# One more product by C on GpSimd, one more product by B per group of states on ScalarE

## What is computed

```python
def _selective_scan(u, delta, A, Bm, Cm, Dp):
    def step(h, inp):
        u_t, d_t, b_t, c_t = inp
        dA = jnp.exp(d_t[:, :, None] * A)
        h = dA * h + (d_t * u_t)[:, :, None] * b_t[:, None, :]
        y = jnp.einsum('bdn,bn->bd', h, c_t)
        return (h, y)
    ...
def _mamba_block(x, p):          # 4 layers; 256 inner channels, 16 states
    xn = _rmsnorm(x, p['norm_w'])
    xp, z = jnp.split(xn @ p['Win'], 2, axis=-1)
    xc = jax.nn.silu(_causal_depthwise_conv(xp, p['conv_w'], p['conv_b']))
    dt, Bm, Cm = jnp.split(xc @ p['Wx'], [DT_RANK, DT_RANK + D_STATE], axis=-1)
    delta = jax.nn.softplus(dt @ p['Wdt'] + p['bdt'])
    y = _selective_scan(xc, delta, -jnp.exp(p['A_log']), Bm, Cm, p['Dp'])
    return x + (y * jax.nn.silu(z)) @ p['Wblk']
```

## Time and profile before

| | |
|---|---|
| median of 3 runs | 2149.23 us (2148.23 to 2153.09) |
| the profiled execution's own time | 2150.92 us |
| its span in the trace | 2149.1 us |
| VectorE busy | 1940.8 us, 90% |
| GpSimd busy | 1457.5 us, 68% |
| ScalarE busy | 1683.6 us, 78% |
| TensorE busy | 1868.8 us, 87% |

### The profile page before, as it was taken

One profiled execution on the slowest core, in us unless ns is written; L12 is line 12 of the kernel. 1 busy time (PEld: TensorE's weight loads), 2 busy tenths in 40 slices (PEclk: granted clock), 3 DMA queues, 4 the chain that ended last, 5 costly groups with the idle time before them and its releaser, 6 DMA issues.

```text
span 2149.1 us, 34575 instructions
## 1 busy us (share of the span) xinstructions
PE 1868.8 (87%) x10784; PEld 1177.3 (55%) x10784; DVE 1940.8 (90%) x1822; ACT 1683.6 (78%) x3053; POOL 1457.5 (68%) x1364
## 2 busy tenths in 40 slices
PE   4688888888888888888888888888888699999998
PEld 2344444444444444444444445444444499998998
DVE  3699999999999999999999999999999987767775
ACT  3799989999899999999999999999999433333333
POOL 2588888888888888888888888888889600000000
PEclk8899999999999999999999999999999999999999
DMA  8333332323232323232323333332322200000000
GB/s 246 75 78 76 77 76 64 78 62 78 62 78 62 78 62 79 65 81 65 81 73 74 81 77 84 74 82 62 78 62 72 84 1 11 11 11 10 10 6 11
DMA packets 73289, 139.45 MB, mean 65 GB/s; under 512 B 13072, under 2 KB 31120, under 8 KB 68624
## 3 DMA queue, kind: packets, MB, share of 16 engines
q1 hardware_dynamic: 66832, 120.32, 23.1%
q10 hardware_dynamic: 6400, 18.42, 3.7%
HBM read 63.85 MB, written 7.74 MB: 33 GB/s over the span
## 4 chain that ended last, share of the span: by engine, by line
POOL 26%; ACT 26%; PE 23%; issue 12%; DVE 3%; ACTq 1%; POOLq 0%; DVEq 0%
POOL scan L469 13%; POOL scan L463 12%; ACT decay L548 11%; PE y_ps L1253 11%; PE dbu_ps L1228 8%; ACT scan L626 6%; DVE scan L814 2%; POOL scan L460 2%; ACT sp_e L585 1%; ACT delta L586 1%; ACT sp_l L595 1%; ACT sp_e L590 1%; PE dbu_ps L1048 1%; ACT du_t L611 1%; PE y_ps L1033 1%
## 5 line engine op out<-in xcount | busy, mean ns | idle before, releaser
L814 DVE TENSOR_TENSOR_SCAN scan<-decay,dbu_ps 128x1024 f32<-128x1024 f32 x512 | 1155.0, 2274 | 41.6 <-PE dbu_ps L1048 36.1
L1048 PE MATMUL dbu_ps<-ident,scan 128*128 128x128 f32 x4096 | 572.0, 286 | 237.4 <-DVE scan L814 200.9
L469 POOL TENSOR_TENSOR scan<-scan,c_rep 128x1024 f32<-128x1024 f32 x255 | 671.9, 2635 | 143.6 <-DVE scan L814 79.0
L1048 PEld LDWEIGHTS dbu_ps<-ident,scan 128*128 128x128 f32 x4096 | 480.2, 146 | 517.8 <-DVE scan L814 266.5
L548 ACT ACTIVATE decay<-d_rep,a_cur 128x510 f32<-128x510 f32 x1024 | 668.0, 709 | 65.0 <-DMA d_rep<-delta 23.6
L463 POOL TENSOR_SCALAR scan<-du_t,b_t 128x256 f32<-128x256 f32 x896 | 594.0, 678 | 0.0
L626 ACT ACTIVATE scan<-du_t,b_t 128x256 f32<-128x256 f32 x1024 | 445.6, 494 | 1.2
L823 DVE TENSOR_TENSOR scan<-scan,c_rep 128x1024 f32<-128x1024 f32 x257 | 332.6, 1294 | 0.0
L751 ACT ACTIVATE decay<-dbu_ps 128x512 f32<-128x512 f32 x256 | 148.1, 597 | 206.1 <-PE dbu_ps L1228 184.1
L1033 PE MATMUL y_ps<-scan,sel 128*32 128x512 f32 x2048 | 298.4, 658 | 0.0
L1061 PE MATMUL pre_ps<-xn,w_pre 128*128 128x512 f32 x512 | 249.8, 611 | 5.5 <-DVE w_pre L803 4.7
(11 more groups left out here) (107 smaller groups left out, 1625.5 us busy)
## 6 DMA issues: line engine op xcount, KB each, us to landing
d_rep<-delta SPq DMA_DIRECT2D x512, 128.0 KB, 2.9
c_rep<-c_rows SPq DMA_DIRECT2D x32, 1024.0 KB
w_pre<-prepared_weights ACTq DMA_DIRECT2D x15, 866.0 KB, 12.6
prepared_weights<-scan SPq DMA_DIRECT2D x3, 1122.0 KB, 13.3
scan<-in_conv_w SPq DMA_DIRECT2D x4, 512.0 KB, 4.8
w_out<-prepared_weights SPq DMA_DIRECT2D x16, 128.0 KB, 12.3
sp_e<-in_x_rows SPq DMA_DIRECT2D x8, 256.0 KB, 3.3
d_rep<-in_w ACTq DMA_DIRECT2D x2, 1024.0 KB, 7.6
```

Source lines behind the costliest of these rows:

```text
L469: nc.gpsimd.tensor_tensor(ring[slot % RING], ring[slot % RING], c_rep[par][:, slot // PRS, :].unsqueeze(1).broadcast_to([128, 2, TG]), ALU ...
L814: nc.vector.tensor_tensor_scan(ring[slot % RING].rearrange("p u t -> p (u t)"), decay[slot % DEC].rearrange("p u a t -> p (u a t)"), dbu_p ...
L1048: last = nc.tensor.transpose(dbu_ps[slot % 2][:, u, 128 * j:128 * j + 128], dbu_t[m % 2][:, j, b, :, :].rearrange("p q c -> p (q c)"), ide ...
```

## The change

Slot 8's product by C goes from VectorE to GpSimd, which then has nine of a window's sixteen and VectorE seven. In exchange GpSimd leaves the last of its eight products by B (q = 3, j = 1) of each group of states to ScalarE, which has nine of sixteen then, three in each of the three slots that hold them, instead of two, three and three (for a step's first group three, three and two). The wait counts follow. The core of the diff:

```diff
+C_POOL = [c for c in range(M * PRS) if c % 2 or c == M * PRS // 2]
+C_DVE = [c for c in range(M * PRS) if c not in C_POOL]
...
-POOL_OUTER = Q * POOL_J
-ACT_OUTER = Q * (JT - POOL_J)
-SHARE = (0, 2, 5, 8)
-FIRST = (0, 3, 6, 8)
+POOL_OUTER = Q * POOL_J - 1
+ACT_OUTER = Q * (JT - POOL_J) + 1
+SHARE = (0, 3, 6, 9)
+FIRST = (0, 3, 6, 9)
...
                 for q, j in itertools.product(range(first, last), range(POOL_J)):
+                    if (q, j) == (Q - 1, POOL_J - 1):
+
+                        continue
...
-                    elif slot % 2 == 0 and slot and has(s, 0):
+                    elif slot - 1 in C_POOL and has(s, 0):
                         times_c(s, i, par, slot - 1)
...
                     q, j = n // (JT - POOL_J), POOL_J + n % (JT - POOL_J)
+                    if n == ACT_OUTER - 1:
+                        q, j = Q - 1, POOL_J - 1
...
-                        if slot % 2:
+                        if slot - 1 in C_DVE:
                             times_c(s, i, par, slot - 1)
...
-                pe.wait_ge(hc_dve, SLOTS // 2 * s + 2 * m + k + 1 + extra)
-                pe.wait_ge(hc_pool, SLOTS // 2 * s + 2 * m + k + 1 - extra)
+                end = PRS * m + 2 * k + 2
+                pe.wait_ge(hc_dve, len(C_DVE) * s + sum(c < end for c in C_DVE) + extra)
+                pe.wait_ge(hc_pool, len(C_POOL) * s + sum(c < end for c in C_POOL) - extra)
```

More of the change, by code:

```diff
@@ L392, in window @@
                     sp.wait_ge(skip_done, STEPS)
-                    sp.wait_ge(hc_dve, SLOTS // 2 * (STEPS - 1))
-                    sp.wait_ge(hc_pool, SLOTS // 2 * (STEPS - 1))
+                    sp.wait_ge(hc_dve, len(C_DVE) * (STEPS - 1))
+                    sp.wait_ge(hc_pool, len(C_POOL) * (STEPS - 1))
                     for e in range(EXPERTS):
@@ L573, in copy_dbc @@
                 act.wait_ge(dbc_ready, s + 1)
-                wait(act, hc_dve, SLOTS // 2 * (s - 1))
-                wait(act, hc_pool, SLOTS // 2 * (s - 1))
+                wait(act, hc_dve, len(C_DVE) * (s - 1))
+                wait(act, hc_pool, len(C_POOL) * (s - 1))
                 act.dma_start(c_dram[par, :, :], dbc[RANK + NS:NBC, :]).then_inc(c_stored, 16)
```

## The result

The changed kernel takes 2177.78 us (median of 4 runs, 2175.89 to 2179.61), the kernel before on the same occasions 2149.89 us (2148.23 to 2153.09): slower by 1.2%, ratio 1.0121 with a 95% interval of 1.0104 to 1.0139. The forecast was 2171 us, with 2155 to 2188 us as the likeliest case's own range. The profiled execution took 2175.89 us, its span is 2174.1 us, 25.0 us more than before.

A forecast was written before the change was run, and what follows sets the result against it. VectorE and an equally long second loop through GpSimd, TensorE and ScalarE were taken to bound the kernel; -1.33 + 2.05 = +0.72 us in 31 windows, less the last window's gain, made +21 us: 2171 us, range 2147 to 2190 us.

The forecast's parts named there:

- the likeliest case: The forecast itself: GpSimd's product of slot 8 stops the last softplus instruction; 2155 to 2188 us, chance 0.72.
- The product of slot 8 gets in between the last two softplus instructions and holds the last: On VectorE, GpSimd's product starts between L849 and L853; L853 ends 2.05 us later, delaying delta and all VectorE work behind.
- VectorE loses 1.33 us a window: VectorE no longer makes slot 8's product by C; from its start to the next scan's is 1.33 us.
- The second loop gets shorter by as much, so that the wait before the softplus stays: Loop from delta over GpSimd, TensorE and ScalarE to the next softplus: 1.2 to 1.5 us shorter, wait stays about 0.73 us.
- the 1.7 that I gave the way up to there: From delta to TensorE at 993.80, up to 1.7 us shorter: 0.46 product by B, 0.57 slot 11, 0.7 ScalarE's copy.
- The 0.7 us in this, for ScalarE's copy behind the first half of the turning: ScalarE's copy at 982.46 came about 0.7 us late behind its decay work, which no longer lies ahead of it.
- A window changes by -1.33 + 2.05: Each window gets 0.72 us longer; 31 windows give 22.3 us, with the last window's gain +21 us.
- ScalarE's products by B cost 0.2 to 0.4 us in the loop, covered: ScalarE's added product by B of group 2, between silu(z) and the logarithm, costs 0.2 to 0.4 us on the second loop.
- Rival A: Slot 8's product on GpSimd delays no one; the second loop limits, 0 to -0.3 us a window, 2141 to 2149 us; chance 0.13.
- B: VectorE alone is the bound and gets back 1.33 us a window, 43 us, 2107 us; chance 0.05.
- C: The loop over ScalarE grows through its wait for d_rep in every other window, 1.4 us in the mean, 2193 us; chance 0.10.

The follow-up runs named there:

- e1_behind_du: The changed kernel, but GpSimd makes the product by C of slot 8 one slot later, behind du: 2149.94 us, 0.9993 of the kernel before.
- e4_halves: The changed kernel, but GpSimd makes slot 8's product as two 128x512 instructions at the same place: 2168.4 us, 1.0088 of the kernel before.
- e7_after_warm: The changed kernel, but TensorE makes the transposes of slot 10 seven times over, filling its wait for scan 9: 2160.67 us, 1.0046 of the kernel before.
- e2_outer_only: Products by B divided as in the changed kernel, products by C as in the kernel before: 2150.36 us, 0.9994 of the kernel before.

## Why the prediction was right, and where it was short

The cause of the loss was forecast rightly. That the time came so near is in part luck: the two terms of the sum gave about half of what was forecast, and a term that was not in it made up for that.

- *The product of slot 8 gets in between the last two softplus instructions and holds the last.* Right. Forecast 3.28 us (1.23 + 2.05), measured 3.26 us; GpSimd's product 1.1 us ahead of its end, measured 1.08; idle time before du 1.1 us, measured 1.16. With the product behind du the loss is gone (e1_behind_du), with half its length the stall is half (e4_halves). By the Trainium skill's rule ("SBUF — State Buffer", "SBUF: two separate sides"), that whoever starts first keeps the port pair for the whole instruction, this was to be expected; the trace agrees, 949 and 2031 ns for a half and a whole. It held in 24 of the 31 windows that I counted with.
- *VectorE loses 1.33 us a window.* Too little: 48.6 us less busy time in products by C, 1.5 us a window, for the seven that are left got shorter as well (mean 1294 ns before, 1262 after).
- *The second loop gets shorter by as much, so that the wait before the softplus stays.* It stays: 34.4 us, before 35.0. But this sign could hardly fail: the wait was 33.7 to 35.2 us in all fourteen kernels, with and without the stall. From the end of delta to silu(z) it took 1002.32 - 975.37 = 26.95 us before and 25.33 after (988.45 to the row below), 1.6 us less, near the 1.7 that I gave the way up to there.

```profile
1013.78 0.60 ACT L569 ACTIVATE sz<-pre_ps 128x512 f32 x1 [0.92 <-PE pre_ps L1079]
```

- The 0.7 us in this, for ScalarE's copy behind the first half of the turning, is misread: the rows give 982.46 - 981.52 = 0.94 us. That the copy then no longer stands behind ScalarE's own work is right; it waited for TensorE 36 times, 32.1 us in all, before 7 times, 8.4 us.
- *A window changes by -1.33 + 2.05.* Too much for these two terms, too little for the window. They gave about 0.4 us and not 0.72, as the windows without a wait at scan 12 show, and those with TensorE's wait filled; in e7_after_warm 10 us are left against the kernel before, where I had summed up 21. The missing term is TensorE's clock. In the trace it is 0.45 us a window (14.0 us over 31): the scans' waits for TensorE, nearly all at scan 12, because the transposes for it stand behind the turning of du at 1.2 GHz. I had the 4.55 us of waiting in the earlier trace rows, and its slow transposes behind it, and took from it only that du was ready in time. With delta 2 us later that wait became 6.6 us, and scan 12 is now due 1.2 us earlier relative to delta (7.7 us behind its end and not 8.9), which took away what hid it. e7_after_warm gives 17 us for it. The 21 us of the sum with these 17 would have given 2188 us, 10 above what was measured.
- *ScalarE's products by B cost 0.2 to 0.4 us in the loop, covered.* Right in that they cost nothing (e2_outer_only, 0.9994).
- Rival A needed L860 at 1.23 us; B a gain of 43 us. Neither came. C was to show in windows that differ by more than 1 us and in a longer wait for d_rep. The windows do differ by up to 1.3 us, but by scan 12's wait for TensorE; ScalarE's wait for d_rep fell from 23.6 us to 12.1 us in all.

## What to carry to other kernels

Work moved to an idle engine is not free if the two engines exclude each other, as VectorE and GpSimd did here: look at what the relieved engine runs in the idle time, instruction by instruction, and above all for a chain of short instructions that wait for one another, since the other engine can get in at any gap. A long instruction there cost nearly its length (2.03 us of 2.36). Place it where the neighbour runs instructions with one SBUF input, and expect that a shift of one engine against the other makes new encounters elsewhere. When a wait of TensorE gets longer, count what it then does at low clock, too. And when a sum comes out right, check its terms one by one: here two of them were off in opposite directions.

## What the runs showed of the hardware

- A product on GpSimd, 128x1024 with two SBUF inputs, holds a VectorE instruction with two SBUF inputs until it has ended: 2031 ns for one of 2.36 us, and 949 ns for a half. VectorE's scans, with one input in PSUM, kept to 2252 to 2289 ns in the changed kernel.
- The gap of 0.03 us between two records of VectorE that wait for one another was enough for GpSimd's product in 26 of 31 windows, in 24 of them ahead of the last softplus instruction (median 3256 ns).
- After 4.55 to 6.68 us of waiting TensorE ran at the 1.2 GHz level for a while: in the kernel before the granted clock was 0.58 in the mean from 977.6 to 981.0 us, in the changed kernel 0.50 for 3.8 us in the window shown. Over 1300 us the mean clock was 1.00 with the wait filled, 0.94 before, 0.93 after and 0.92 with the product alone moved.
